# Expert layers of a small macaron network: the last 32 middle columns multiplied for four steps at a time instead of two

## What is computed

```python
logits = xt @ gate_w.T                         # xt: 1024 x 512, E = 8 experts
top_vals, top_idx = top_k(softmax(logits), 2)  # K = 2
h1 = einsum('th,efh->tef', xt, w1)             # F = 800 middle columns
h3 = einsum('th,efh->tef', xt, w3)
act = silu(h1) * h3
expert_out = einsum('tef,ehf->teh', act, w2)
y = einsum('te,teh->th', w_full, expert_out)   # x = x + 0.5 * y
```

## Time and profile before

| | us |
|---|---|
| median of 3 runs | 1270.81 (1269.35 to 1272.06) |
| span of the profiled execution | 1260.5 |
| TensorE busy | 1174.8 (93%) |
| VectorE busy | 870.9 (69%) |
| ScalarE busy | 354.5 (28%) |
| first MoE layer, up(0) to the last y | about 197.7 to 501 |
| second MoE layer | about 927.6 to 1239.7 |

### The profile page before, as it was taken

One profiled execution on the slowest core, in us unless ns is written; L12 is line 12 of the kernel. 1 busy time (PEld: TensorE's weight loads), 2 busy tenths in 40 slices (PEclk: granted clock), 3 DMA queues, 4 the chain that ended last, 5 costly groups with the idle time before them and its releaser, 6 DMA issues.

```text
span 1260.5 us, 28155 instructions
## 1 busy us (share of the span) xinstructions
PE 1174.8 (93%) x9962; PEld 509.8 (40%) x9962; DVE 870.9 (69%) x2483; ACT 354.5 (28%) x746; POOL 139.2 (11%) x191
## 2 busy tenths in 40 slices
PE   6799988999999999899899999998979899999992
PEld 3478563333333332444344444433634233333330
DVE  5822676887777773577989999941559577777763
ACT  5434611000000001223177767774110000000010
POOL 2200011111110001343000000000111011011000
PEclk9899979999999999999999999999999999999996
DMA  9100333268724345428504442005841655515556
GB/s 360 52 1 1 155 144 121 54 204 278 253 75 139 106 146 193 167 79 179 147 3 85 61 60 35 2 2 214 339 166 40 254 168 194 194 51 198 185 183 243
DMA packets 63668, 174.33 MB, mean 138 GB/s; under 512 B 9885, under 2 KB 16627, under 8 KB 61351
## 3 DMA queue, kind: packets, MB, share of 16 engines
q1 hardware_dynamic: 55471, 150.60, 37.3%
q0 software_dynamic: 5760, 18.88, 4.4%
q10 hardware_dynamic: 2296, 3.05, 0.7%
HBM read 785.47 MB, written 22.03 MB: 641 GB/s over the span
## 4 chain that ended last, share of the span: by engine, by line
PE 80%; DVE 9%; DMA 4%; ACT 3%; issue 2%; SPq 1%; POOL 0%; ACTq 0%; POOLq 0%; DVEq 0%
PE PS L1096 30%; PE PS L1115 14%; PE PS L1595 6%; PE PS L1582 5%; PE PS L1558 5%; PE PS L817 3%; PE PS L801 2%; PE PS L1622 2%; PE PS L1510 2%; PE PS L581 2%; PE PS L1129 1%; PE PS L1515 1%; DVE PS L1716 1%; PE PS L1585 1%; PE PS L565 1%
## 5 line engine op out<-in xcount | busy, mean ns | idle before, releaser
L1096 PE MATMUL PS<-arena 128*32 128x400 f32 x3456 | 396.9, 502 | 8.0 <-DMA HH<-in_w 4.1
L1096 PE MATMUL PS<-HH,arena 128*32 128x400 f32 x1152 | 396.3, 502 | 0.0
L1096 PEld LDWEIGHTS PS<-arena 128*32 128x32 f32 x3456 | 143.6, 110 | 255.0 <-issue 247.1
L1286 DVE STREAM_TRANSPOSE arena<-arena 32x192 f32<-32x192 f32 x576 | 211.5, 367 | 7.2
L1716 DVE CUSTOM_DVE_ANT_0 PS<-PS,U 128x128 f32<-128x128 f32 (+7 forms) x256 | 188.7, 783 | 15.3 <-PE PS L1558 12.7
L1115 PE MATMUL PS<-arena 128*32 128x512 f32 x1512 | 195.5, 600 | 4.0 <-DVE arena L1286 4.0
L1663 ACT ACTIVATE arena<-PS 128x512 f32<-128x512 f32 (+3 forms) x384 | 160.9, 497 | 63.6 <-PE PS L1585 49.0
L1264 DVE STREAM_TRANSPOSE arena<-arena 32x128 f32<-32x128 f32 x544 | 164.7, 303 | 15.5 <-DMA arena<-h_scratch,RT 7.6
L1169 ACT ACTIVATE arena<-PS 128x400 f32<-128x400 f32 x72 | 36.2, 503 | 434.7 <-PE PS L1096 434.7
L1270 DVE TENSOR_TENSOR arena<-arena,PS 128x400 f32<-128x400 f32 x72 | 40.9, 571 | 136.1 <-ACT arena L1169 136.1
L1096 PEld LDWEIGHTS PS<-HH,arena 128*32 128x32 f32 x1152 | 125.4, 110 | 0.0
(11 more groups left out here) (255 smaller groups left out, 1250.3 us busy)
## 6 DMA issues: line engine op xcount, KB each, us to landing
arena<-in_w SPq DMA_DIRECT2D x456, 800.0 KB
arena<-in_w2a SPq DMA_DIRECT2D x266, 768.0 KB
HH<-in_w SPq DMA_DIRECT2D x152, 800.0 KB
HH<-in_w2a SPq DMA_DIRECT2D x38, 768.0 KB
arena<-split_scratch SPq DMA_DIRECT2D x96, 128.0 KB, 6.5
arena<-y_scratch SPq DMA_DIRECT2D x24, 256.0 KB, 5.5
split_scratch<-arena SPq DMA_DIRECT2D x8, 768.0 KB, 4.6
arena<-in_w2b SPq DMA_DIRECT2D x72, 64.0 KB
```

What stands on the lines that cost most here:

```text
L1096: mm = eng.matmul(PS[SR * j:SR * j + SR, 2 * hf + m, 0:FH], XBT[:, u, c, SR * j:SR * j + SR], W13[j][:, c // 2, m, c % 2, hf * FH:(hf + 1) ...
L1286: tr = eng.transpose(ACT_T[SR * b:SR * b + SR, u, :, rows], src[:, :, SR * b:SR * b + SR])
```

## The change

The last 32 middle columns are multiplied for four steps at a time (steps 0 to 3, 4 to 7, 8 to 11, 12 to 15); steps 16 and 17 stay alone. After down's L1115 of the fourth step, 16 matmuls are issued, four for each stream, in 16 different 32 x 32 places. To hold four open outputs, bank 4 + p % 4 takes the place of bank 4 + p % 2; `ACT_R` becomes a ring of eight in its own tensor; `W2B` gets two more places, in `VBR` and `wu1T`, which earlier layers used. ScalarE copies four outputs after every fourth step, still through two `YB` places, and GpSimd scatters four in a row. `tail_in` waits for the step four back.

```diff
+QUAD = 4
+        ACT_RING = sb("ACT_RING", [P, 2 * QUAD * SR])
-        ACT_R = take([4, SR])
+        ACT_R = ACT_RING[:].rearrange("p (a t) -> p a t", a=2 * QUAD)
-        W2B = [take([D]), U]
+        W2B = [take([D]), U, VBR, wu1T[:].rearrange("p c t -> p (c t)")]
+        take([4, SR])
+        GROUPED = (NSTEP - 1) // QUAD * QUAD
-        def paired(p):
-            return p < NSTEP - 2
+        def grouped(p):
+            return p < GROUPED
         def y_done(p):
-            return p + 2 if paired(p) and p % 2 == 0 else p + 1
+            return p // QUAD * QUAD + QUAD if grouped(p) else p + 1
+        def y_bank(p):
+            return 4 + p % QUAD
         def last_rows(p, j):
-            r = (j + p % 2) % NSTR
+            r = (j + p % QUAD) % NSTR
...
-                    if q >= 2:
-                        eng.wait_ge(S("m_y"), NSTEP * f + y_done(q - 2))
+                    if q >= QUAD:
+                        eng.wait_ge(S("m_y"), NSTEP * f + y_done(q - QUAD))
...
+            done = 0
             for p in range(2, NSTEP):
                 gather(p)
-                if p >= 5 and p % 2 == 1:
-                    scatter(p - 5)
-                    scatter(p - 4)
-            for p in range(NSTEP - 4, NSTEP):
+                if p % QUAD == QUAD - 1 and p >= 2 * QUAD - 1:
+                    for q in range(done, done + QUAD):
+                        scatter(q)
+                    done += QUAD
+            for p in range(done, NSTEP):
                 scatter(p)
...
-                if G >= 2:
-                    eng.wait_ge(S("m_yc"), G - 1)
+                if G >= QUAD:
+                    eng.wait_ge(S("m_yc"), NSTEP * f + max(p - QUAD + 1, 0))
...
-                if paired(p) and p % 2 == 0:
+                if y_done(p) > p + 1:
                     return
-                ends = (p - 1, p) if paired(p) else (p,)
+                ends = range(p - QUAD + 1, p + 1) if grouped(p) else (p,)
...
-                        mm = eng.matmul(PS[SR * j:SR * j + SR, 4 + q % 2, :], ACT_R[rows, (NSTEP * f + q) % 4, :],
-                                        W2B[q % 2][rows, :], start=False, stop=True, skip_group_check=True)
+                        mm = eng.matmul(PS[SR * j:SR * j + SR, y_bank(q), :], ACT_R[rows, (NSTEP * f + q) % (2 * QUAD), :],
+                                        W2B[q % QUAD][rows, :], start=False, stop=True, skip_group_check=True)
...
-                if p >= 1 and not paired(p - 1):
+                if p >= 1 and not grouped(p - 1):
                     ready = (p - 1,)
-                elif p >= 2 and p % 2 == 0:
-                    ready = (p - 2, p - 1)
+                elif p >= QUAD and p % QUAD == 0:
+                    ready = range(p - QUAD, p)
```

More of the change, by code:

```diff
@@ L946, in tail_in @@
         def tail_in(eng, p, j, e):
-            eng.dma_start(W2B[p % 2][last_rows(p, j)], A["w2b"][e].rearrange("e p d -> p (e d)")).then_inc(w2b_in[p % 2], 16)
+            eng.dma_start(W2B[p % QUAD][last_rows(p, j)], A["w2b"][e].rearrange("e p d -> p (e d)")).then_inc(w2b_in[p % 2], 16)
         def guess(j):
@@ L1114, in down @@
                     for j in range(NSTR):
-                        mm = eng.matmul(PS[SR * j:SR * j + SR, 4 + u, :], ACT_T[:, u, c, SR * j:SR * j + SR],
+                        mm = eng.matmul(PS[SR * j:SR * j + SR, y_bank(p), :], ACT_T[:, u, c, SR * j:SR * j + SR],
                                         half_of(j, half)[:, c % (FC // 2), :], start=(c == 0), stop=False,
@@ L1180, in act_moe @@
                         eng.wait_ge(y_out[u], 16 * (NSTEP // 2 * f + q // 2))
-                    eng.copy(YB[:, u, :], PS[:, 4 + u, :]).then_inc(S("m_yc"), 1)
+                    eng.copy(YB[:, u, :], PS[:, y_bank(q), :]).then_inc(S("m_yc"), 1)
             if f == 1:
@@ L1282, in dve_moe @@
                     rows = slice(SR * a, SR * a + SR)
-                    eng.transpose(ACT_R[last_rows(p, a), G % 4, :], AC[rows, FC * P:FF])
+                    eng.transpose(ACT_R[last_rows(p, a), G % (2 * QUAD), :], AC[rows, FC * P:FF])
                     for b in range(NSTR):
```

## The result

The changed kernel takes 1259.81 us (median of six), the kernel before 1272.49 us (median of six; three of them are the runs of the table above): a ratio of 0.990, 95% interval 0.9879 to 0.9921. The forecast was 1263.2 us with a range of 1260.6 to 1267.8. Repeated, the pair gave 0.9893 (0.9879 to 0.9907), and on one further occasion, against the same executions of the kernel before, 0.9917 (0.9885 to 0.9949) and 0.9911 (0.9880 to 0.9942). Over everything timed, 120 executions of the kernel before average 1269.3 us and 22 of the changed one 1258.4: a gain of 10.9 us, with an uncertainty of 1.3 (two standard errors). The forecast had 7.65. Three slow executions (2771.81 us of the kernel before, 3074.75 and 1762.86 us of two experiments) stand in the medians given here, but in no ratio and no mean.

The account below looks back on a forecast made before the run. TensorE, busy 93% of the span, was taken as the bound, its own sequence unbroken through the MoE layers. Terms: - 9.2 + 0.4 + 1.15 = - 7.65 us, from 1270.81 to 1263.2 us; range 1260.6 to 1267.8.

Parts of the forecast that it names:

- The visits removed: TensorE's visits to L1129 in both MoE layers: eight disappear at 1.15 us each, 9.2 us saved.
- The sixteen places: Each of eight remaining visits holds 16 matmuls instead of eight: 1.07 us instead of 1.02, 0.4 us added in all.
- Two waves: Rival: the array takes eight matmuls at a time, so a visit lasts 1.9 us; 1269.6 us in all, chance 0.11.
- four turns: Rival: four row groups cannot write one stream's PSUM partitions at once; a visit lasts 3.6 us, total 1283.4, chance 0.05.
- The visit given back in up(4): Second layer: without the visit after down(1), up(4) comes sooner but its weight chunks do not; 1.15 us becomes idle time.
- The waits: Sign: up(4) of the second layer should wait 1.15 us longer for its weights.
- The copies in fours: ScalarE's four copies together, the third waiting for the first scatter to land, 4.1 us after issue at the median: cost nothing.
- the 4.0 us named: Up's lead covering a late Silu: the product ends at 254.98, the up needing it starts at 258.96.
- "Nothing": SyncE: tail_in waits less often, and the fourth step's tail rows are still issued one step ahead; no cost.
- "I take nothing for it": Lower clock in up(4)'s last chunk, second layer: a longer pause may start it sooner, but the next wait hides it; zero.
- The 1261.6 named for its lower side: Time given for the case that up(4) gives the visit back and the extra matmul starts cost nothing.

Follow-up runs that it names:

- with the places taken away: Changed kernel with last_rows turned by p % 2, so a visit's 16 matmuls share eight places, two in each: 1263.48 us, ratio 0.9952.
- the moved instructions: Changed kernel with SyncE's value loads for the next step, and tail_in in three steps of four, before the wait for down's second half: 1258.8 us, 0.9898.
- The third profile of the kernel before: Kernel before, unchanged, run once more on a further occasion: 1268.66 us, ratio 1.0007.
- before, again: Kernel before, unchanged, run again for its spread: 1269.84 us, ratio 1.000.
- tail_in alone: Kernel before with only the four W2B places and tail_in waiting for the step four back: 1269.55 us, ratio 0.9975.
- only down(17) filled: Eight bf16 matmuls put ahead of down(17) in both layers: kernel before 1269.7 us (0.9989), changed kernel 1260.83 (0.9919).
- the pauses filled: Both kernels with eight matmuls ahead of down(17) in both layers, six ahead of up(4)'s last chunk in layer two: 1268.65 us (1.0009) and 1260.58 (0.9950).

## Why the prediction came out as it did

**The visits removed: right.** 1.15 us each was the term. In the changed kernel a cycle of four steps takes 15.92 + 15.90 + 15.89 + 17.10 = 64.81 us, where two cycles of two took 2 x (15.92 + 17.03) = 65.90. That is 1.09 us per removed visit with the dearer visit already in it; the forecast had 1.15 - 0.05 = 1.10.

**The sixteen places: right.** 1.07 us was forecast for a visit, 1.08 is shown, and with the places taken away 1.92 against the rival's 1.9. *Two waves* and *four turns* are out.

**The visit given back in up(4): right in size, half wrong in cause.** With the visit and without it the stretch takes 53.5 and 53.7 us. But SyncE's wait for down(1) held the loads by 0.9 us at most; SyncE itself was late, as the moved instructions showed. The waits did not grow by 1.15 us, in part because the loads came 0.7 us sooner for the reason below.

**The copies in fours: right that they cost nothing, wrong in the landing.** 4.1 us was taken; beside loads it is 7.4, with Silu 0.8 us late and covered by the 4.0 us named.

**What was missing.** Seven visits at 1.09 make 7.63 us, the forecast's sum to 0.02. The measured gain is 10.9 us, uncertain by 1.3. A first piece of the rest is 0.7 us: with copies and scatters in fours no scatter stands ahead of the value loads for step 4. The forecast put SyncE at "Nothing", but for a shorter wait, and did not ask what GpSimd's moved scatters do to SyncE. That step failed, by 0.7 us, and this is shown. The third profile of the kernel before, at the higher clock throughout, has 54.4 us from up(2) to up(5), the changed kernel 53.7.

The second piece is the granted clock after a pause: "I take nothing for it". That step failed too, as a bound rather than as a value. In the last chunk of up(4) the lower clock costs 1.4 us (4.26 against 2.89) and was low in three of five profiles of kernels in which visits, loads and scatters stand as before (before, again, tail_in alone; not the third, not with only down(17) filled), in none of the four of the changed kernel. In down(17) it costs 1.7 us. Over all profiles with pauses not filled, it was low in 8 of 12 layers with the visits of before and in 3 of 16 with fewer or in fours. With those counts the forecast's sum becomes 7.65 + 0.7 + 0.8 (1.4 x 3/5) + 1.6 (1.7 x 2 x (8/12 - 3/16)) = 10.8 us.

That this comes near the measured 10.9 shows nothing, for three reasons. It leaves out the place that speaks the other way: up(0) of the first layer was slow in 4 of 8 profiles with the visits of before and in 9 of 10 of the others, all four of the changed kernel among them, by 1.1 to 2.5 us. It costs 0.8 us on average in the eight and 1.6 in the ten; counted in, that takes 0.8 us off again. The granted clock also falls outside the two layers (0.50 from 524.2 to 527.5 us in the first profile of the kernel before), where nothing was counted. And with the pauses filled the kernel before should have fallen by some 3 us. It moved by - 0.1% and + 0.1%, while the changed kernel became slower: 1260.55 us over 13 executions against 1258.4, uncertain by 1.9. So it is on the side of the changed kernel that the gain of 10.9 shrinks to 8.4, which is not what the reading of the clock had said.

What is shown is 8.3 us: the stages at like clock have it, the forecast's 7.65 and the 0.7, and so have the two kernels with the pauses filled (8.4, uncertain by 1.9). Shown too is that the low clock meets both kernels, and that filling the pause removes it from down(17). The 2.6 us above that, uncertain by 1.3, stay open. They may be the clock by the changed kernel's timing, the clock by the draw, or something outside the layers, and so it stays open whether the lasting gain is nearer to 8 or to 11 us.

**The range** was the practical fault. Executions of one kernel spread by some 3 us about their mean (1262.6 to 1278.3), and a draw of the clock worth up to 4.8 us per execution was in the rows (PEclk 0.75 in the earlier trace rows, the 0.89 us passes in the earlier trace rows). A floor 2.6 us under the forecast left it no room on the side of the gain. The 1261.6 named for its lower side is 1270.81 - 9.2 and holds only where up(4) takes nothing of the saved visit; with that visit lost to the waits and the starts free it is 1262.8. And the first comparison itself drew well, 12.7 us, 1.8 more than the mean of all: had it drawn the 8.3 us of the stages, 1262.5, the time would have lain inside the range.

## What to carry to other kernels

Where small contractions are collected for the places of the array, what counts is the number of visits: one costs about the same with four, eight or sixteen float32 matmuls in it (1.03, 1.02, 1.08 us), as long as every matmul has a place of its own. Before counting a removed stretch as gain, look for the next wait for a load whose issue does not move with it, and look at whose instructions come just ahead of that issue. Where TensorE pauses for 2 to 3 us in a kernel, as here ahead of down(17) and of the last chunk of up(4), put the lower clock after it into the range on both sides, for every such place and not only for those where it helps the change, and compare kernels by stages, since one profile may differ from the next by more than the change.

## What the runs showed of the hardware

Sixteen float32 matmuls of 32 x 32 weights and 512 columns, in sixteen places and four PSUM banks, start within 0.11 us and are done as fast as four: 1.08 against 1.04 us. Two in one place take turns: 1.92.

SyncE's value loads out of SBUF take 0.27 us, and two of four took 0.68 and 0.57 when GpSimd had issued two scatters just before; moved some 7.5 us later, behind the value loads, the scatters cost them nothing (0.27 to 0.28). Why is not tested.

After one and the same pause of 1.98 us, in the same kernel at the same place, the next 48 records took 5.3 us at a granted clock of 1.00, or 7.0 at 0.76. The pause alone doesn't decide it.
